# A two-layer graph network: layer 0's first norm taken per node ahead of the gathers

## The reference, cut to what matters

```python
h = relu(layernorm(x))                                  # per node
agg = segment_sum(h[src], dst)                          # sum over a node's incoming edges
x = x + agg @ W_rel.T + b_rel + h @ W_root.T            # layer 0
h = relu(layernorm(x))
w = silu(edge_attr @ We1 + be1) @ We2 + be2             # per edge, 50 -> 128 -> 128
agg = segment_sum(h[src] * w, dst)
x = x + h + silu(agg @ Wn1 + bn1) @ Wn2 + bn2           # layer 1
```

## Time and profile before

| | |
|---|---|
| median of 3 runs | 4972.77 us (4953.61 to 4975.04) |
| profiled execution | 4927.46 us, span 4925.0 us |
| PE, DVE, ACT, POOL busy | 2588.1, 1954.1, 1186.6, 2980.9 us |
| granted TensorE clock, mean | 0.638 of full speed |
| DMA | 285.33 MB, 58 GB/s |
| first and last gather of layer 0 issued | 3.52 and 2382.47 us |
| first and last gather of layer 1 issued | 2484.03 and 4849.70 us |

### The profile page before, as it was taken

The page is one execution under the profiler, slowest core; times in us unless marked ns, Lnnn a source line. Parts: engine busy times, 40 slices in busy tenths (PEclk is TensorE's granted clock), DMA queues, the critical chain, the costliest instruction groups (busy, mean ns, idle before and its releaser), DMA issues.

```text
span 4925.0 us, 49782 instructions
## 1 busy us (share of the span) xinstructions
PE 2588.1 (53%) x10958; PEld 1971.2 (40%) x10958; DVE 1954.1 (40%) x6931; ACT 1186.6 (24%) x2732; POOL 2980.9 (61%) x3135
## 2 busy tenths in 40 slices
PE   1333333333333333333436768677777777676777
PEld 0333333333333332333324445455545455454555
DVE  3344444443444444444523333333333333333334
ACT  1333333333333333333401111111111111111111
POOL 7566666666666666666265666666666666665662
PEclk9555555555555555555556777766777777767777
DMA  2111211112111121111122222222222222222221
GB/s 70 49 49 53 55 49 50 50 52 54 50 51 50 50 57 51 49 50 50 35 61 62 65 68 68 65 64 64 68 64 68 62 66 69 67 64 63 67 68 53
DMA packets 205872, 285.33 MB, mean 58 GB/s; under 512 B 67828, under 2 KB 135462, under 8 KB 205618
## 3 DMA queue, kind: packets, MB, share of 16 engines
q0 software_dynamic: 100096, 205.20, 16.1%
q10 hardware_dynamic: 62434, 61.11, 4.3%
q1 hardware_dynamic: 43216, 17.95, 1.4%
HBM read 263.58 MB, written 20.45 MB: 58 GB/s over the span
## 4 chain that ended last, share of the span: by engine, by line
another core or an unknown queue 30%; PE 26%; DVE 18%; issue 17%; DVEq 5%; ACT 4%; ACTq 0%; DMA 0%; POOL 0%; SPq 0%; POOLq 0%
PE seg_a L305 8%; PE seg_b L305 4%; DVE e_stats L588 4%; PE ew_a L351 4%; DVEq L579 3%; PE ew_b L351 3%; PE hid_a L345 3%; PE hid_b L345 3%; ACT rows L413 2%; DVE onehot L572 2%; DVE e_mv L592 2%; DVE agg L583 2%; DVE ew_a L673 1%; DVE rows L680 1%
## 5 line engine op out<-in xcount | busy, mean ns | idle before, releaser
L276 POOL DMA_INDIRECT rows<-h_rows,idx x1564 | 1490.9, 953 | 976.4 <-issue 537.7
L276 POOL DMA_INDIRECT rows<-x,idx x1564 | 1489.0, 952 | 892.7 <-issue 479.7
L305 PE MATMUL seg_a<-onehot,rows 128*128 128x128 f32 x3312 | 746.7, 397 | 1354.3 <-ACT rows L413 514.4
L305 PEld LDWEIGHTS seg_a<-onehot,rows 128*128 128x128 f32 x3312 | 657.7, 295 | 1447.1 <-issue 1141.1
L305 PE MATMUL seg_b<-onehot,rows 128*128 128x128 f32 x2944 | 626.5, 381 | 572.6 <-DVE onehot L572 269.7
L413 ACT ACTIVATE rows<-rows,e_shift,e_rstd 128x128 f32<-128x128 f32 x1564 | 643.3, 481 | 907.8 <-DVE e_shift L599 719.8
L305 PEld LDWEIGHTS seg_b<-onehot,rows 128*128 128x128 f32 x2944 | 557.0, 282 | 648.6 <-issue 461.9
L572 DVE TENSOR_TENSOR onehot<-iota_ps,dst_rel 128x512 f32<-128x512 f32 x782 | 532.5, 681 | 1.4
L583 DVE TENSOR_TENSOR agg<-seg_a,agg 128x128 f32 x414 | 119.8, 289 | 760.4 <-remote 393.3
L494 ACT ACTIVATE hidden<-hid_a,be_col 128x512 f32<-128x512 f32 x208 | 142.9, 687 | 1137.4 <-remote 522.6
L351 PEld LDWEIGHTS ew_a<-we_sb,hidden 128*128 128x128 f32 x1664 | 272.8, 248 | 309.0 <-ACT hidden L494 184.2
(11 more groups left out here) (102 smaller groups left out, 1712.4 us busy)
## 6 DMA issues: line engine op xcount, KB each, us to landing
rows<-x,idx POOLq DMA_INDIRECT x1564
rows<-h_rows,idx POOLq DMA_INDIRECT x1564
ef_a<-ef_blocks ACTq DMA_DIRECT2D x70, 300.0 KB
ef_b<-ef_blocks ACTq DMA_DIRECT2D x47, 300.0 KB
xs<-x SPq DMA_DIRECT2D x26, 256.0 KB
y_rows<-ys ACTq DMA_DIRECT2D x26, 256.0 KB
ys<-y_rows SPq DMA_DIRECT2D x26, 256.0 KB
out<-xs ACTq DMA_DIRECT2D x26, 256.0 KB
```

Of the source, the lines that this page charges most:

```text
L276: pool.indirect_dma_start(out=rows[:, u, t, :], out_offset=None, in_=table, in_offset=bass.IndirectOffsetOnAxis(ap=idx[:, j:j + 1], axis=0 ...
L305: mm = pe.matmul(seg[u % 2][:, 0:P], rows[:, u, t, :], onehot[:, u % HOT, t, :], start=(t == 0), stop=(t == TB - 1))
```

## The change

A stage ahead of the blocks normalises every node once. It works through 25 groups of 512 nodes, five at a time, in a loop of five rounds:

- SP loads a group of `x` (`load_h`); DVE takes statistics and factors (`stats_h`, `shift_of`); ACT takes the root and writes relu(norm) (`std_h`, `relu_h`).
- SP stores the group to a new table `h_rows` in DRAM (`store_h`).
- PE turns it, and DVE (three groups of five) or ACT (two of five) copies the turned group into `h_table`. That is the memory of `agg[1]`, which layer 1 clears later.

POOL still gathers pass 0 from the raw `x`, beside this stage, and the blocks of pass 0 are normalised as before. Before pass 1 POOL waits until all of `h_rows` is stored. From pass 1 on it gathers from `h_rows`, PE waits for the landed rows (`s_rows`), and no per-edge norm is left. The node update of layer 0 takes its turned group from `h_table`: its first norm and its transposes are gone from all 26 updates. Clearing `agg[0]` and the plan of the windows now come after the new stage on DVE; SP issues the weight loads earlier. Before layer 1 DVE also waits for the last read of `h_table` before it clears `agg[1]`. Layer 1 is unchanged but for where one buffer of edge features lies.

```diff
+H_SETS = 5
+assert GROUPS % H_SETS == 0
+H_BY_ACT = (3, 4)
...
+    h_rows = nc.dram_tensor("h_rows", (N_PAD, D), F32, kind="Internal").ap()
...
+        hs, h1s = work_sets(0)[0], work_sets(1)
+        hT, aggT = flat(node_sets("hT", 3)), flat(work_sets(2))
+
+        ef = [sb("ef_a", [D_EDGE, EF_BLOCKS, BLOCK])[:, :, :], node_work[0:D_EDGE, :, :]]
...
+        h_table = agg[1]
+        h_x = [xs[:, 0, :, :], xs[:, 1, :, :], xs[:, 2, :, :], hs, h1s[0]]
+        h_out = [ys[:, 0, :, :], ys[:, 1, :, :], ys[:, 2, :, :],
+                 *(s.rearrange("p (t f) -> p t f", t=TB) for s in (hT[0], aggT[0]))]
+        h_turn = [*hid_ps, *ew_ps, seg[0]]
...
@@ -196,7 +217,22 @@
+            def load_h(k, r):
+                sp.dma_start(h_x[r], node_group(x, k * H_SETS + r)).then_inc(s_hx[r], 16)
+
+            def store_h(k, r):
+                hold(sp, s_hh, k * H_SETS + (r + 1))
+                sp.dma_start(node_group(h_rows, k * H_SETS + r), h_out[r]).then_inc(s_hstore[r], 16)
+
+            for r in range(H_SETS):
+                load_h(0, r)
             sp.dma_start(dst_sb[:, :, :], dst_cols.rearrange("p (k t) -> p k t", t=TB)).then_inc(s_dst, 16)
...
@@ -208,11 +244,16 @@
+            with sp.Fori(0, GROUPS // H_SETS - 1) as k:
+                for r in range(H_SETS):
+                    store_h(k, r)
+                    load_h(k + 1, r)
+            for r in range(H_SETS):
+                store_h(GROUPS // H_SETS - 1, r)
+            for r in range(H_SETS):
+                hold(sp, s_hstore[r], 16 * (GROUPS // H_SETS + 1))
+            hold(sp, s_hturn, GROUPS)
...
@@ -279,8 +319,12 @@
             with pool.Fori(0, passes_so_far) as p:
-                with pool.Fori(0, ITERS) as it:
-                    gather(0, x, p * ITERS + it, 0)
+                gather(0, x, p * ITERS, p * ITERS)
+                for r in range(H_SETS):
+                    hold(pool, s_hstore[r], 16 * (GROUPS // H_SETS + 1))
+                with pool.Fori(1, ITERS) as it:
+                    i = p * ITERS + it
+                    gather(0, h_rows, i, i)
...
@@ -289,16 +333,31 @@
+            with pe.Fori(0, GROUPS // H_SETS) as k:
+                for r in range(H_SETS):
+                    n = k * H_SETS + r
+                    pe.wait_ge(s_hcopy[r], k + 1)
+                    pe.wait_ge(s_hh, n + 1)
+                    for t in range(TB):
+                        tr = pe.transpose(h_turn[r][:, t * P:(t + 1) * P], h_out[r][:, t, :], ident[:, :])
+                    tr.then_inc(s_hturn, 1)
+            for r in range(H_SETS):
+                hold(pe, s_hcopy[r], GROUPS // H_SETS + 1)
...
@@ -307,12 +366,6 @@
-                def transpose():
-                    pe.wait_ge(s_nh, n + 1)
-                    for t in range(TB):
-                        tr = pe.transpose(node_t[r][:, t * P:(t + 1) * P], hs[r][:, t, :], ident[:, :])
-                    tr.then_inc(s_nhT, 1)
...
@@ -321,17 +374,26 @@
-                return {7: transpose, 9: product}
+                return {9: product}
...
-                with pe.Fori(0, ITERS) as it:
+                    pe.wait_ge(s_onehot[0], i * U + (u + 1))
+                    pe.wait_ge(s_h, p * U + (u + 1))
+                    pe.wait_ge(s_acc[0], slot_free(i, u, 2))
+                    segment_sum(0, u)
+                with pe.Fori(1, ITERS) as it:
...
                         pe.wait_ge(s_onehot[0], i * U + u + 1)
-                        pe.wait_ge(s_h, i * U + u + 1)
+                        pe.wait_ge(s_rows[0][u], i * (16 * TB) + 16 * TB)
                         pe.wait_ge(s_acc[0], slot_free(i, u, 2))
                         segment_sum(0, u)
...
@@ -399,45 +461,73 @@
+            with act.Fori(0, GROUPS // H_SETS) as k:
+                def std_h(r):
+                    act.wait_ge(s_hstats, k * H_SETS + (r + 1))
+                    nc.scalar.activation(e_std[:, r, :], e_mv[:, r, :, 1], ACT.Sqrt,
+                                         bias=eps[:, :]).then_inc(s_hstd, 1)
+
+                def relu_h(r):
+                    act.wait_ge(s_hshift, k * H_SETS + (r + 1))
+                    act.wait_ge(s_hcopy[r], k + 1)
+                    act.wait_ge(s_hstore[r], k * 16 + 16)
+                    for t in range(TB):
+                        op = nc.scalar.activation(h_out[r][:, t, :], h_x[r][:, t, :], ACT.Relu,
+                                                  bias=e_shift[:, r, t:t + 1], scale=e_rstd[:, r, t:t + 1])
+                    op.then_inc(s_hh, 1)
+
+                std_h(0)
+                for r in range(H_SETS):
+                    if r + 1 < H_SETS:
+                        std_h(r + 1)
+                    relu_h(r)
+                for r in H_BY_ACT:
+                    act.wait_ge(s_hturn, k * H_SETS + (r + 1))
+                    nc.scalar.activation(h_table[:, bass.ds(k * (H_SETS * BLOCK) + r * BLOCK, BLOCK)],
+                                         h_turn[r][:, :], ACT.Copy).then_inc(s_hcopy[r], 1)
...
@@ -448,20 +538,24 @@
-                return {4: lambda: node_std(n, r, 0), 6: lambda: node_relu(hs[r], n, r, 0), TURN_AT: turned,
-                        11: lambda: node_std(n, r, 1), 13: h1, 15: y, 16: stored}
+                return {TURN_AT: turned, 11: lambda: node_std(n, r), 13: h1, 15: y, 16: stored}
...
+                edge_std(p * U, 0)
+                    edge_relu(p * U, u)
+                    if u + 1 < U:
+                        edge_std(p * U, u + 1)
+                with act.Fori(1, ITERS) as it:
...
-                    edge_std(i, 0)
                     for u in range(U):
                         if u in steps:
                             steps[u]()
-                        edge_relu(i, u)
-                        if u + 1 < U:
-                            edge_std(i, u + 1)
...
@@ -534,6 +628,39 @@
+            with dve.Fori(0, GROUPS // H_SETS) as k:
+                def stats_h(r):
+                    dve.wait_ge(s_hx[r], k * 16 + 16)
+                    stats_of(h_x[r], r, s_hbn, k * H_SETS + (r + 1), s_hstats)
+
+                def copy_h(r):
+                    dve.wait_ge(s_hturn, k * H_SETS + (r + 1))
+                    v.tensor_copy(h_table[:, bass.ds(k * (H_SETS * BLOCK) + r * BLOCK, BLOCK)],
+                                  h_turn[r][:, :]).then_inc(s_hcopy[r], 1)
+
+                stats_h(0)
+                for r in range(H_SETS):
+                    if r + 1 < H_SETS:
+                        stats_h(r + 1)
+                    shift_of(r, s_hstd, s_hrecip, s_hshift, k * H_SETS + (r + 1))
+                    if r >= 2:
+                        copy_h(r - 2)
             v.memset(agg[0][:, :], 0.0)
...
@@ -628,31 +741,43 @@
+                    dve.wait_ge(s_nx, loaded * 16)
...
-                return {2: stats_x, 4: lambda: node_shift(n, r, 0), 9: x1, 11: lambda: node_shift(n, r, 1), 13: y}
+                return {9: x1, 11: lambda: node_shift(n, r), 13: y}
 
             window_targets().then_inc(s_setup, 1)
             dve.wait_ge(s_setup, 9)
+            hold(dve, s_hh, GROUPS)
+            for r in range(H_SETS):
+                hold(dve, s_hcopy[r], GROUPS // H_SETS + 1)
             with dve.Fori(0, passes) as p:
...
+                edge_stats(p, 0)
+                edge_stats(p, 1)
+                edge_shift(p, 0)
...
+                with dve.Fori(1, ITERS) as it:
                     i = p * ITERS + it
                     steps = node_update0(i, 0, i + 1)
-                    edge_stats(i, 0)
-                    edge_stats(i, 1)
-                    edge_shift(i, 0)
                     for u in range(U):
                         dve.wait_ge(s_seg[0], slot_free(i, u, HOT))
                         one_hot(0, it, u)
-                        if u + 2 < U:
-                            edge_stats(i, u + 2)
-                        if u + 1 < U:
-                            edge_shift(i, u + 1)
                         add_window(0, i, it, u)
                         if u in steps:
                             steps[u]()
...
@@ -662,11 +787,11 @@
+            hold(dve, s_nT, updates(passes, n_late))
             v.memset(agg[1][:, :], 0.0)
```

More of the change, by code:

```diff
@@ L70, in build @@
         base_all = sb("base_all", [P, BLOCKS_PAD], I32)
-        hi_row = agg[1][0:1, BLOCKS_PAD // P * BLOCK:BLOCKS_PAD // P * BLOCK + BLOCKS_PAD].bitcast(I32)
+        hi_row = sb("hi_row", [1, BLOCKS_PAD], I32)
         base_row = sb("base_row", [1, BLOCKS_PAD], I32)
@@ L144, in build @@
         s_mout, s_out = sem("s_mout"), sem("s_out")
+        s_hx = [sem(f"s_hx{r}") for r in range(H_SETS)]
+        s_hbn, s_hstats, s_hstd, s_hrecip = sem("s_hbn"), sem("s_hstats"), sem("s_hstd"), sem("s_hrecip")
+        s_hshift, s_hh, s_hturn = sem("s_hshift"), sem("s_hh"), sem("s_hturn")
+        s_hcopy = [sem(f"s_hcopy{r}") for r in range(H_SETS)]
+        s_hstore = [sem(f"s_hstore{r}") for r in range(H_SETS)]
         block = ctx.enter_context(nc.Block())
@@ L265, in _, with gather @@
             pool.reg_mov(passes_so_far, 1)
```

(37 more changed lines are left out.)

117 lines of the change are left out of this document (69 added, 48 removed).

## The result

The changed kernel takes 4905.26 us (median of 4 runs, 4895.94 to 4910.27), the kernel before beside it 4965.75 (4953.61 to 4975.04): ratio 0.987, 95% interval 0.9846 to 0.9894. That is 60 us less, where 39 were forecast. The sign came as forecast. The front's cost, the passes' gain and the tail's gain were all sized too small, and the holds behind the first two are of another kind than I had pictured.

A forecast was written before the change was run, and what follows sets the result against it. No engine is full; late PE signals hold DVE and POOL, 103.7 us a pass against POOL's 85.0. +41 - 67 - 4 - 8.8 = -39 us; with the runs' 45.3 us offset 4934, range 4770 to 5015.

The forecast's parts named there:

- The front: New stage beside pass 0: it ends at 120 us, so pass 2 starts at 248 instead of 206.93, +41 us.
- holds: Stretches where engines get awaited signals late, PE's some 7 us, while POOL issues gathers; about every three blocks in both layers.
- The passes: Passes 2 to 22 of layer 0 fall from 103.7 to 100.5 us each: -67 us, bounds 0 and -393.
- 3 us a pass for the turn: Instruction fetch at the turn of DVE's loop: by that rule alone 63 us gained in 21 passes.
- rival A: Holds shrink, POOL need not stop and passes near 85 us; at 90 us a pass 4713 us; chance 0.16.
- With one hold a round ...: New stage: 3.4 rounds done in 77 us, the other 1.6 after POOL falls silent; stage ends at 110 us.
- With two holds a round ...: New stage: only 1.7 rounds done before POOL falls silent; stage ends at 131 us.
- I take 120: End of the new stage in us, taken between 110 (one hold a round) and 131 (two).
- my bound of 139: End of the new stage in us with three holds a round, which makes the front +60 us.
- Tail and late groups: Layer 0 after its last gather: -4 us (bounds 0 and -10); first norm of three late node groups gone: -8.8 us.
- Layer 1 (0): Layer 1 unchanged at 102 us a pass: 0 us, the moved buffer being loaded at the same place.
- The long gather: Gather of 7.23 us under DVE's memset; the new order frees 6 us of POOL in pass 0, outside the sum.

The follow-up runs named there:

- e5: Changed kernel with six PSUM banks instead of two and five one-hots instead of three in layer 0, one-hots made four blocks ahead; 4846.45 us, ratio 0.9768.
- e1: Kernel before without the per-edge norm of the gathered rows, with no new stage; 4850.47 us, ratio 0.9786.
- e8: Changed kernel with VectorE's ten edge-norm instructions back in every block of passes 1 to 22, on constants, results unread; 4961.78 us, ratio 1.0.
- e7: Changed kernel with ScalarE's five edge-norm instructions back in every block of passes 1 to 22, on constants, results unread; 4921.12 us, ratio 0.9903.
- e2: Changed kernel with the per-edge norm back in every pass of layer 0, gathering from x; 4953.26 us, ratio 0.9989.
- e12: Changed kernel with each block's one-hot in passes 1 to 22 made by four instructions instead of one; 4922.91 us, ratio 0.9944, on a chip with holds.
- e3: Changed kernel with POOL waiting for the end of the new stage before its first gather; 4917.5 us, ratio 0.9896.
- e4: Changed kernel with POOL's pass 0 gathers dealt out: two blocks, then two after each stage round, the last five after the plan; 4880.15 us, ratio 0.9808.

## Why the prediction was right in kind and wrong in size

**The passes (forecast 21 x 3.2 = -67; measured -80 and -92): the step of the sum that was mis-sized most in the change's favour.** I argued that the norm hides behind PE and that only the start of a pass comes free, and took a middle between the bare pace within a pass (98.8) and layer 1 (102.2). The start itself came as argued. VectorE at the turn of a pass, first the add in the kernel before that follows the one at 1029.21, then the changed kernel:

```profile
1039.69 0.29 DVE L583 TENSOR_TENSOR agg<-seg_a,agg 128x128 f32 x1 [1.94 <-PE seg_a L305]
...
1059.10 0.29 DVE L710 TENSOR_TENSOR agg<-seg_a,agg 128x128 f32 x1 [2.34 <-PE seg_a L364]
1059.73 0.69 DVE L699 TENSOR_TENSOR onehot<-iota_ps,dst_rel 128x512 f32<-128x512 f32 x1 [0.35 <-issue]
1062.95 0.29 DVE L710 TENSOR_TENSOR agg<-seg_a,agg 128x128 f32 x1 [2.52 <-PE seg_a L364]
...
1075.48 0.29 DVE L710 TENSOR_TENSOR agg<-seg_b,agg 128x128 f32 x1 [11.64 <-remote]
```

From the last add of a pass to the first of the next, the mean of 20 turns is 11.0 us before and 3.9 now: the 7 us of the prediction. But the other 16 blocks went from 92.8 to 95.9 us, with a long wait now just behind the turn, where my middle only mixed two paces.

What the runs showed in place of that middle: the parts do not add. Without the edge norm a pass costs 99.5, without the node group's first norm and transpose 101.4, without both 99.9. I read some 99.5 as the floor for this depth of buffers, since e5 moves it.

Of the 4.2 to 4.8 us a pass that e1 gains, e8 gives back 1.9 with VectorE's ten instructions, their fetches and their wait for rows, e7 0.4 with ScalarE's five, within the scatter. The prediction worked out 3 us a pass for the turn by the Trainium skill's rule ("Runtime: NRT & Kernel Launch", "Instruction fetch mechanics") that a taken branch to a page not held has to be fetched first. The trace agrees that the idle time and the fetches go together (some 3 us and 121 fetches before, 0.35 us and 15 fetches now); in e8 they came back for less than 3 us a pass, so the rule may hold all of e8's 1.9, but not e2's 2.3 to 2.9, which come with all fetches kept. The run that adds working instructions to VectorE and no fetch (e12; 15 fetches on its page) costs 0.6. I had counted the first norm of a node group as part of the start of a pass; e2, with the fetches and the edge norm kept, shows it to be worth more than half of the gain alone. In e7 the turn takes 9.1 us and the other 16 blocks 91.2, at nearly the same pace, so where in a pass the time stands does not tell what a part costs. What share of the gain each cause has is not shown. POOL's pauses over 1.5 us in passes 2 to 22 fell from 115 to 89 and from 357 to 291 us in all, still every three to five blocks: the holds shrank a little, as in rival A, and stopped far from its 90 us a pass.

**The front (forecast +41, bounds to +60; measured +61).** The step that failed is the count of holds in the stage ("With one hold a round ...", "With two holds a round ...", "I take 120"): I priced one or two holds a round of some 22 us each, whatever stands between the waits. In its place the runs showed waits that grow with the number of instructions between one signal and the next. VectorE in the first round, and the end of the stage, changed kernel:

```profile
21.81 0.38 DVE L637 BATCH_NORM_AGGREGATE e_mv<-e_stats 128x2 f32<-128x6 f32 x4 [4.18 <-remote]
22.11 0.15 DVE L642 RECIPROCAL e_rstd<-e_std 128x4 f32<-128x4 f32 x1
28.73 0.16 DVE L644 SCALAR_TENSOR_TENSOR e_shift<-e_mv,e_rstd 128x4 f32<-128x4 f32 x1 [6.48 <-remote]
29.27 0.69 DVE L654 COPY agg<-hid_a 128x512 f32 x1 [0.38 <-issue]
29.88 0.86 DVE L633 BATCH_NORM_STATS2 e_stats<-node_work 128x6 f32<-128x128 f32 x4
37.20 0.38 DVE L637 BATCH_NORM_AGGREGATE e_mv<-e_stats 128x2 f32<-128x6 f32 x4 [6.46 <-remote]
...
127.94 0.69 DVE L654 COPY agg<-ew_a 128x512 f32 x1 [0.20 <-PE ew_a L355]
140.59 0.69 DVE L654 COPY agg<-ew_a 128x512 f32 x1 [0.21 <-PE ew_a L355]
143.89 10.72 DVE L664 MEMSET agg<- 128x12800 f32 x1 [2.62 <-issue]
```

From 21.81 to 28.73 stand four aggregates and a reciprocal: 5 x 1.40 = 7.0, and 6.92 us pass. From 28.73 to 37.20 a factor, a copy and four statistics: 6 x 1.40 = 8.4, and 8.47 us pass. Of the ten such stretches up to 96 us six come out within 0.1 us; four are off by 0.7 to 1.5, two either way, so the count is an estimate there. Only two rounds were done by 103 us; the last three, with POOL silent, took 12.65 us each (my 13). The stage ended at 141, past my bound of 139 and past the 130 that the prediction itself named as the sign of being wrong. Memset, plan and first block took 28 us, not 24, and pass 1 98.9, not 103.7.

**Tail and late groups (forecast -4 and -8.8; measured -11.8 and -10.7 against the first profile of before).** Timeline of VectorE after the last gather (answers to the earlier trace rows):

```profile
2376.85 0.29 DVE L710 TENSOR_TENSOR agg<-seg_a,agg 128x128 f32 x1 [2.34 <-PE seg_a L364]
2380.07 0.29 DVE L710 TENSOR_TENSOR agg<-seg_b,agg 128x128 f32 x1 [2.34 <-PE seg_b L364]
...
2418.71 0.29 DVE L710 TENSOR_TENSOR agg<-seg_a,agg 128x128 f32 x1 [2.34 <-PE seg_a L364]
```

Blocks of 3.2 us as forecast; but the last add comes 54 us behind the last gather, not 62: the node update, for which I added 6, stands beside the blocks.

**Layer 1 (0)** was right. Its scatter of over 40 us from run to run makes 22 of the 31 us by which the first profile of before lies under the second.

**The long gather.** The prediction put the 7.23 us gather under a memset down to a rule of the Trainium skill ("SBUF — State Buffer", "Who interferes with whom"), by which an instruction of VectorE in a two-port mode shuts GpSimd out. The rows repeat the wait: a gather under a memset of 10.72 us took 12.51 us in the changed kernel and 10.00 in e3. Which mode a memset runs in no run here shows, so the rule is not shown to be the reason. Gathers beside the stage's copies out of PSUM stayed at 0.94 to 0.95 us, as was expected.

**Together.** The front's cost was forecast 20 too small, the passes' gain 13 to 25 and that of tail and late groups 9: the errors partly cancelled, which is luck, and left -48 by the profiles. The remaining 12 us to the -60 of the medians are within the scatter of runs.

## What to carry to other kernels

Where another engine issues gathers without a pause, count the instructions between two waits and not only their time. In a bare chain of waits each cost 1.40 us there, however small; in this layer, where POOL's waits for slots set the pace, three more a block cost 0.6 us a pass. Work that is moved to the front should be tried with the gathers dealt out between its rounds (e4) before its cost is taken for given. And profile the kernel before more than once when the gain sought is 1%.

## What the runs showed of the hardware that I had not expected

While POOL issues indirect gathers back to back (1.25 us each), the copies of VectorE and of ScalarE go over to turns of 1.40 us each (on VectorE with 512 columns or with one); rows of 128 bytes or gathers of 64 rows change nothing in that, and waits after every 8 gathers kept all links free. Nops take no turn. VectorE and ScalarE each had their own turns in the same 1.40 us. TensorE was not timed in such a chain, so that its signals come 7 us late in the earlier trace rows for the same reason is argued and not shown. One chip of five shows none of this: 3992 us for the kernel before instead of 4951 to 4971, with the same gathers of 0.95 us. What differs there, and what the turns are, was not found. Every run here, the timed ones too, was recorded; whether the turns belong to the recording was not tried.
